# All inverse roots in one GpSimd power instruction each, in place of twelve VectorE instructions

## The reference

```python
def _layernorm(x, axis=-1, eps=1e-05):
    m = jnp.mean(x, axis=axis, keepdims=True)
    v = jnp.var(x, axis=axis, keepdims=True)
    return (x - m) / jnp.sqrt(v + eps)
# in the second attention, on q and k, 32 heads of 8 columns:
    def _rmsnorm(t):
        return t * jax.lax.rsqrt(jnp.mean(t * t, axis=-1, keepdims=True) + EPS)
...
x = x + _L0_xattn_ref(_layernorm(x, axis=-1), ctx_2048, ctx_2048, ...)   # 16 heads, rotary, softmax
x = x + _L0_ffn_ref(_layernorm(x, axis=-1), ...)      # 16 experts of 128, top 2 of 2 groups; shared 512
x = x + _L1_xattn_ref(_layernorm(x, axis=-1), ctx_2048, ...)             # 32 heads, q and k normed
x = x + _L1_ffn_ref(_layernorm(x, axis=-1), ...)      # base matmul plus top-2 of 16 low-rank experts
```

## Time and profile before

| | before |
|---|---|
| median of 3 runs | 474.33 us (473.31 to 475.53) |
| the profiled execution | 475.81 us |
| its span in the profile | 474.0 us |
| busy: TensorE, VectorE | 375.1 us, 325.5 us |
| busy: ScalarE, GpSimd | 175.3 us, 64.5 us |
| mean granted TensorE clock | 0.903 of full |

### The profile page before, as it was taken

One profiled execution on the slowest core, in us unless ns is written; L12 is line 12 of the kernel. 1 busy time (PEld: TensorE's weight loads), 2 busy tenths in 40 slices (PEclk: granted clock), 3 DMA queues, 4 the chain that ended last, 5 costly groups with the idle time before them and its releaser, 6 DMA issues.

```text
span 474.0 us, 7584 instructions
## 1 busy us (share of the span) xinstructions
PE 375.1 (79%) x2754; PEld 222.0 (47%) x2754; DVE 325.5 (69%) x893; ACT 175.3 (37%) x237; POOL 64.5 (14%) x151
## 2 busy tenths in 40 slices
PE   5257677378877867999999999999869777486895
PEld 4113233233333324466666667666545445354363
DVE  8875578479888647285545537586785877868785
ACT  1104446155565641143343333433453434432001
POOL 0323424244342200000000000000000000000000
PEclk9755889899999976999999999999995978977899
DMA  7551642626655120000000000225025454540011
GB/s 241 149 173 58 182 132 72 198 70 203 193 188 175 66 78 0 1 0 0 2 0 0 1 0 0 76 82 143 14 72 163 129 147 127 168 136 1 1 46 44
DMA packets 61971, 41.81 MB, mean 88 GB/s; under 512 B 3952, under 2 KB 59760, under 8 KB 61936
## 3 DMA queue, kind: packets, MB, share of 16 engines
q1 hardware_dynamic: 61360, 41.10, 28.6%
q10 hardware_dynamic: 576, 0.23, 0.2%
HBM read 26.71 MB, written 14.42 MB: 87 GB/s over the span
## 4 chain that ended last, share of the span: by engine, by line
PE 51%; DVE 32%; issue 7%; DMA 5%; ACT 3%; POOL 2%; DVEq 0%; POOLq 0%
PE psum L627 13%; PE psum L640 13%; DVE mx L1169 6%; DMA qstk<-mT 5%; PE psum L534 4%; PE psum L715 4%; PE psum L615 3%; PE psum L498 2%; PE psum L519 2%; DVE stats L1144 2%; ACT prob L880 2%; DVE rope_ab L1158 2%; DVE rs_a L1133 1%; DVE rs_a L1132 1%; PE psum L483 1%
## 5 line engine op out<-in xcount | busy, mean ns | idle before, releaser
L1169 DVE TENSOR_REDUCE mx<-psum 128x2 f32<-128x512 f32 x128 | 81.1, 683 | 25.4 <-PE psum L498 24.5
L880 ACT ACTIVATE prob<-psum 128x1024 f32<-128x1024 f32 x64 | 64.1, 1022 | 73.7 <-PE psum L519 73.6
L1381 DVE SCALAR_TENSOR_TENSOR xall<-psum,comb,xall 128x256 f32<-128x256 f32 x128 | 53.1, 477 | 41.5 <-PE psum L640 41.1
L627 PE MATMUL psum<-xnT,wup 128*128 128x512 f32 x160 | 76.2, 600 | 0.0
L640 PE MATMUL psum<-wdn,act 128*128 128x256 f32 x320 | 75.5, 379 | 0.6 <-DVE xall L1378 0.6
L640 PEld LDWEIGHTS psum<-wdn,act 128*128 128x128 f32 x320 | 60.7, 190 | 25.9 <-issue 19.1
L929 ACT ACTIVATE rel<-psum 128x512 f32<-128x512 f32 x40 | 23.9, 597 | 97.3 <-PE psum L627 97.3
L330 POOL TENSOR_TENSOR parts<-qk_rest,parts 128x512 bf16<-128x512 f32 x15 | 17.3, 1156 | 229.9 <-ACT parts L955 225.0
L534 PE MATMUL psum<-prob,vt 128*32 128x256 f32 x512 | 39.1, 424 | 6.4 <-ACT prob L880 5.8
L985 ACT ACTIVATE prob<-psum 128x1024 f32<-128x1024 f32 x32 | 32.6, 1024 | 25.8 <-PE psum L737 25.8
L627 PEld LDWEIGHTS psum<-xnT,wup 128*128 128x128 f32 x160 | 30.2, 194 | 22.7 <-issue 21.0
(11 more groups left out here) (153 smaller groups left out, 470.8 us busy)
## 6 DMA issues: line engine op xcount, KB each, us to landing
qstk<-stack_scratch SPq DMA_DIRECT2D x32, 256.0 KB, 3.7
kstk<-stack_scratch SPq DMA_DIRECT2D x32, 256.0 KB, 4.4
stack_scratch<-parts SPq DMA_DIRECT2D x32, 192.0 KB, 2.1
stack_scratch<-parts SPq DMA_DIRECT2D x32, 128.0 KB, 2.1
wup<-in_wup SPq DMA_DIRECT2D x4, 640.0 KB, 6.4
wdn<-in_wdn SPq DMA_DIRECT2D x4, 640.0 KB, 8.0
stack_scratch<-parts SPq DMA_DIRECT2D x32, 64.0 KB, 1.8
out<-xall SPq DMA_DIRECT2D x8, 128.0 KB, 1.7
```

Source lines behind the costliest of these rows:

```text
L627: last = nc.tensor.matmul(psum[:, n % 2, :], wup[:, f, BLOCKS[g], :], xnT[:, f, c * HALF:(c + 1) * HALF], start=(f == 0), stop=(f == 1))
L880: nc.scalar.activation(prob[(b * PAIRS + k) % 3][:], exp_buf(k).rearrange("p a n -> p (a n)"), ACT.Exp, scale=SCALE).then_inc(exp_done, 1)
L1169: nc.vector.tensor_reduce(mx[:, half, :, 4 * s + p4:4 * s + p4 + 1], bank.rearrange("n (b m) -> n b m", b=2), AX_X, ALU.max).then_inc(misc ...
L1381: last = nc.vector.scalar_tensor_tensor(out=xall[:, b, :], in0=src, scalar=comb[:, b, e:e + 1], in1=xall[:, b, :], op0=ALU.mult, op1=ALU.add)
```

## The change

Every inverse root moves from VectorE to GpSimd, as two instructions: a scale and add of the variance, and a power of it with exponents from a tile that holds -0.5 (`half_power`, set once). VectorE signals `var_ready` with the instruction that ends the variance and waits for `rsqrt_done` before it goes on. GpSimd's queue gets the sixteen roots at fixed places between its other work: before the rotation of batch 1, between rest and third of batch 1, around its last division in stage A, then in stages B to D between the thirds. GpSimd's loop over the thirds is written out, and so is VectorE's loop over slots 1 to 4. The tile `rs_a` goes.

```diff
-        rs_a = sb("rs_a", [P, 64])
+        half_power = sb("half_power", [P, 64])
...
+            roots = iter(range(1, 100))
+
+            def root(o, var, scale, eps, n):
+
+                pool.wait_ge(var_ready, next(roots))
+                steps.then(nc.gpsimd.tensor_scalar(rs_v[:, 0:n], var, scale, eps, ALU.mult, ALU.add))
+                nc.gpsimd.tensor_tensor(o, rs_v[:, 0:n], half_power[:, 0:n], ALU.pow).then_inc(rsqrt_done, 1)
+
+            def rstd_of(first, n):
+                root(rstd[:, first:first + n], mv[:, first:first + n, 1], 1.0, LN_EPS, n)
+
+            def rs_of():
+                root(rs[:], ss[:], 1.0 / HD, RMS_EPS, 64)
+
+            nc.gpsimd.memset(half_power[:], -0.5).then_inc(init, 1)
             nc.gpsimd.memset(zeros[:], 0.0).then_inc(init, 1)
-            pool.wait_ge(init, 1)
+            pool.wait_ge(init, 2)
+            rstd_of(0, FIRST)
             nc.gpsimd.drain().then_inc(qk_ready, 1)
             for b in range(1, 3):
                 rotate(PROLOGUE.index(("q", b)) + 1)
                 if b < 2:
                     rest(b, b)
+                    rstd_of(FIRST, NB - FIRST)
                     third(b, b)
...
+            rstd_of(0, B_EARLY)
             divide(NB - 1)
-
-
-            with pool.Fori(0, 4) as i:
-                for par in range(2):
-                    third(NB + 2 * i + par, par)
+            rstd_of(B_EARLY, NB - B_EARLY)
+
+
+            rstd_of(0, 4)
+            for b in range(2):
+                rs_of()
+                third(NB + b, b)
+            rs_of()
+            rstd_of(4, 4)
+            for b in range(NB):
+                if b + 2 < NB:
+                    third(NB + b + 2, b % 2)
+                if b == 5:
+                    rstd_of(0, 4)
+                if b + 3 < NB:
+                    rs_of()
+            rstd_of(4, 4)
...
-            def rsqrt(o, var, scale, eps, n):
...
+            roots = iter(range(1, 100))
+
+            def root_of(ins):
+
+                ins.then_inc(var_ready, 1)
+                dve.wait_ge(rsqrt_done, next(roots))
...
-                steps.then(last)
-                rsqrt(rstd[:, first:first + n], mv[:, first:first + n, 1], 1.0, LN_EPS, n)
+                root_of(last)
...
-                    steps.then(nc.vector.tensor_reduce(
+                    root_of(nc.vector.tensor_reduce(
                         ss[:].unsqueeze(2), sq[:].rearrange("n (h d) -> n h d", d=HD), AX_X, ALU.add))
-                    rsqrt(rs[:], ss[:], 1.0 / HD, RMS_EPS, 64)
...
-            with dve.Fori(0, 2) as i:
-                steps.enter(i, 2 * (1 + 12 + 4))
-                for b0 in (1, 2):
-                    slot_c(b0, i, 1)
-            steps.leave(2)
+            for b in range(1, 5):
+                slot_c(b, 0, 1)
```

More of the change, by code:

```diff
@@ L40 @@
 RH = 64
-RSQRT_GUESS = 0x5F3759DF
 class Steps:
@@ L202, in build @@
         egap_done = sem("egap_done")
+        var_ready = sem("var_ready")
+        rsqrt_done = sem("rsqrt_done")
         dve_step = sem("dve_step")
```

## The result

The changed kernel takes 533.13 us (median of 4 runs, 531.74 to 535.29) against 474.86 us of the kernel before: ratio 1.1236, 95% interval 1.1187 to 1.1286. It is 12% slower; the forecast was 460.2 us in a range of 451 to 482.

A forecast was written before the change was run, and what follows sets the result against it. No engine was full; in the second attention TensorE and VectorE take turns, nothing covering the root. Layernorm roots 7.0, per-head roots 5.6 and prologue 1.5 us sum to 14.1 off the 474.33 us median: 460.2 us, range 451 to 482.

The forecast's parts named there:

- Where the roots lie, and what is removed: On the path: per-head roots of slots 0 to 4, 3.05 us each; four layernorm roots, 2.41 each; the prologue's apart.
- What is added without the power: Hops between VectorE and GpSimd, scale-and-add and its wait: 0.39 us a root at 4 columns, 0.47 at 64.
- The power: GpSimd's second instruction of each root: 20 ns per column over 190 ns, so 0.27 us at 4 columns, 1.47 at 64.
- three constructions: Power's price per column: twelve removed steps, 23 ns; by VectorE's reciprocal, 18 ns; logarithm and exponential of twelve steps each, 45.
- the rival: Same as Rival (1): a slow power on GpSimd, at 75 ns per column 479 us in all, at 100 ns 487 us.
- The sum: Four layernorm roots gain 7.0 us, five per-head roots 5.6, the prologue 1.5: 14.1 us off the median, 460.2 us.
- The formula of the rival: Gain by the power's price p per column: (7.3 - 0.02p) + (12.0 - 0.32p) + 1.5; nil at p = 61.
- The cover: Expert stage: per-head roots hidden under full TensorE, costed at nothing; cover of 1.6 us, gone at a power over 4.2 us.
- The prologue: `xn` starts near 20.0 us in place of 22.50; row maxima start some 1.5 us before 25.93, no more.
- The clock as a gain: Second attention: with a shorter wait for `qkn` one fall of TensorE's clock may stay away, up to 3 us, not summed.
- Rival (1): A slow power on GpSimd, VectorE and TensorE behind it: 0.5% slower from 68 ns per column, 487 us at 100; chance 0.23.
- The others: Cheap power, 454 to 457 us, 0.17; middling, 465 to 477, 0.13; gain given back, 467 to 473, 0.06; first call, 0.05.
- a loaded code: First power on GpSimd slow alone as code or a table is loaded: 461.5 us or some 466 us; chance 0.05.

The follow-up runs named there:

- the product: The changed kernel with a product in place of the power in all sixteen roots, so the roots are not computed; 458.43 us, ratio 0.9693.
- 24-column run: The changed kernel with the per-head power on 24 of 64 columns, the other roots left out and read as 1; 475.13 us.
- 32-column run: The changed kernel with the per-head power on 32 of 64 columns, the other roots left out and read as 1; 488.72 us.

## Why the prediction was wrong

**Where the roots lie, and what is removed.** Right in the main. All five per-head roots of the slots and the layernorm roots named were on the path; 3.05 and 2.41 us were the lengths to beat. The layernorm root at the end of the first attention has six columns, not four, and went from 2.46 to 1.75 us only; and the 1.0 us that the root of the last stage gained was taken by the clock, as shown above.

**What is added without the power.** Right to 0.03 us: 0.44 us measured for 0.47, and the product's root of 0.77 us for 0.78.

**The power.** This step failed. I took p = 20 ns per column between three constructions from the add's rate and VectorE's reciprocal, with 45 as the end of the range and 75 to 100 as the rival. It is 159 ns, 84 times the add's 1.89. The text itself said that no row bars more, and yet closed the upper end by counting arithmetic steps, for which it had no row. The rule of the Trainium skill (GPSIMD Engine Reference, Performance pitfalls for Q7 kernels), 4 cycles for each step of a dependent fp32 chain, pointed the right way, but the twenty steps that I put into it gave 67 ns; at its 4 cycles a step and 1.2 GHz, 159 ns would be an estimate of 48 steps in a row. No run shows the instruction's inside.

**The sum.** The formula of the rival holds with the right p: (7.3 - 0.02 x 159) + (12.0 - 0.32 x 159) + 1.5 = -33.3 us, which is 507.6 us. The slot stretch lost 36.9 us against 5 x 7.94 less 1.0 for the root at 342 us = 38.7.

**The cover.** The missing 25.5 us are the second half of the expert stage. The prediction named the condition, a power of over 4.2 us, and then left the three roots out of the rival's price all the same; with p = 75 or 100 (powers of 5.0 and 6.6 us) it should have reached them as well. The 24-column run (4.17 us) confirms the bound from below, the 32-column run (5.43 us) is past it; the 1.6 us lie among the covers measured at the three roots, 2.5, 1.8 and 1.4. What I had not foreseen is that a wait of 5.5 us brings TensorE's clock down, so that even the covered part is lost.

**The prologue.** The first maxima start at 25.05, 0.9 us earlier, not 1.5. The power of six columns takes 1.34 us, and `xn` starts at 20.79, not at 20.0; that is still 1.7 us earlier than before. But this one `xn` takes 1.24 us in place of 0.41, beside GpSimd's third part of batch 1 (20.73 to 21.88):

```profile
20.79 1.24 DVE L1174 TENSOR_SCALAR xn<-xall,mv,rstd 128x256 f32<-128x256 f32 x1 [2.46 <-POOL rstd L1056]
```

The bound of 1.5 us from the stack's arrival was wrong too: in the product kernel `xn` starts at 19.32 and takes 0.41 us, and the maxima start at 22.76, 3.2 us earlier than before, of which only 0.6 us had been gained ahead of this root.

**GpSimd's queue.** Right: no root stood behind other work except in the prologue, and the third parts were done before each. In the prologue the third part stood behind the root, as the prediction said it would for one over 0.7 us: its input was there at 19.69 and it started at 20.73.

**The clock as a gain.** A fall less was allowed for in the lower end. At the end of the first attention (166.53 to 185.42 us before, 165.25 to 181.70 after) 2.4 us were gained where the root is 0.7 shorter, with a granted clock of 0.90 in place of 0.65. In the slots the sign is not predictable from the wait's length: the product removes the waits for `qkn` whole and still has a slot at 0.76.

**The rivals.** Rival (1) named mechanism and place and had a chance of 0.23, but its price stopped at 487 us. The others, a loaded code among them, did not occur: the first power (5.4 us, 2 columns) took 0.71 us, the other of that shape 0.70.

## What to carry to other kernels

Before an operation is moved, look for its price per column on the new engine; where no row shows it, the range has no upper end, and one instruction of it at two widths, put anywhere, settles it. GpSimd's power, at 0.38 us and 159 ns a column, beats the twelve VectorE instructions up to about 10 columns ((2.41 - 0.39 - 0.38) / 0.159, from the layernorm root's length and what stands around the power) and loses beyond some 14 (the same with 3.05 and 0.44 of the per-head root). A wait that cover hides is hidden up to a length only, here 1.4 to 2.5 us, and past it the clock can take back the covered part as well.

## What the runs showed of the hardware

GpSimd's power of two fp32 operands takes 702, 1010, 1336, 2902, 4166, 5430 and 10549 ns at 2, 4, 6, 16, 24, 32 and 64 columns. On 8 partitions it takes what it takes on 128 (10539 ns), and a square takes what an inverse root takes (10551). A product of the same shape takes 319 ns.

The hand-over VectorE to GpSimd and back with two short instructions between (scale-and-add, product) costs 0.6 us for 4 columns and 0.77 for 64, so short dependent chains of VectorE are worth moving when GpSimd has the operation cheaply.

TensorE's granted clock fell behind a wait of 5.48 us in a stage that had been at 1.00 throughout, and stayed at its lower level until 4.4 us after the wait's end (0.50 up to 302.5 us); behind waits of 0.36 and 1.01 us it did not.

Some VectorE instructions that start beside a GpSimd one end only with it. `xn` of 128x256 at 20.79 us takes 1.24 us in place of 0.41 and ends at 22.03, beside a GpSimd instruction that ends at 21.88. In the product kernel `nmean` at 19.65 us takes 1.12 us where it takes 0.16 in the changed kernel; it ends at 20.77, the GpSimd instruction beside it at 20.74.
